# Mamba-2 decay matrices built as an offset minus an absolute difference, with Abs and Exp in place in PSUM

## What is computed

```python
def _ssd(xh, dt, A, Bm, Cm):
    cum = jnp.cumsum(dt * A, axis=1)
    diff = cum[:, :, None, :] - cum[:, None, :, :]
    decay = jnp.where(mask[None, :, :, None], jnp.exp(diff), 0.0)
    scores = jnp.einsum('bln,bsn->bls', Cm, Bm)[..., None] * decay * dt[:, None, :, :]
    return jnp.einsum('blsh,bshp->blhp', scores, xh)

def _mamba2(x, Win, Wconv, bconv, dt_bias, A_log, D, gn_w, Wout):
    zxbcdt = x @ Win                       # z, x, B, C, dt
    xBC = silu(causal_conv(...))           # x 128 wide, B and C 16 wide
    dt = softplus(zxbcdt[..., -NHEADS:] + dt_bias)
    y = _ssd(xh, dt, A, Bm, Cm) + rev(_ssd(rev(xh), rev(dt), A, rev(Bm), rev(Cm)))
    y = y + D * xh
    y = _rmsnorm(y.reshape(b, l, DIN) * silu(z), gn_w)
    return y @ Wout
```

## Time and profile before

| | |
|---|---|
| time, median of 3 runs | 2949.18 us (2942.47 to 2951.99) |
| profiled execution | 2953.49 us, of it 2951.5 us span from first to last instruction |
| granted TensorE clock, mean | 0.857 of full speed |
| busy: TensorE, VectorE, ScalarE, GpSimd | 2153.9, 1981.8, 1744.2, 1079.7 us |
| the first block begins | 904.9 us into the span |
| the eighth block | 2680.4 to 2929.1 us |

### The profile page before, as it was taken

One profiled execution on the slowest core, in us unless ns is written; L12 is line 12 of the kernel. 1 busy time (PEld: TensorE's weight loads), 2 busy tenths in 40 slices (PEclk: granted clock), 3 DMA queues, 4 the chain that ended last, 5 costly groups with the idle time before them and its releaser, 6 DMA issues. The chain is left out here.

```text
span 2951.5 us, 64266 instructions
## 1 busy us (share of the span) xinstructions
PE 2153.9 (73%) x26182; PEld 1100.1 (37%) x26182; DVE 1981.8 (67%) x2779; ACT 1744.2 (59%) x2811; POOL 1079.7 (37%) x827
## 2 busy tenths in 40 slices
PE   4277777776774887698688588658857886885886
PEld 3022222222221553354255245325524542552553
DVE  2587888888877566565666656565765666666564
ACT  1266766766653575477367457536754773674574
POOL 0044444444451343244045235304522531451342
PEclk6588888888896998799799799869978988997998
DMA  4000000000001111110111111011111101111111
GB/s 133 0 0 1 0 1 0 1 0 0 1 0 29 32 34 28 35 33 15 44 38 26 38 27 40 15 31 32 34 36 26 42 15 39 33 25 30 32 34 31
DMA packets 96695, 74.59 MB, mean 25 GB/s; under 512 B 69392, under 2 KB 77584, under 8 KB 95120
## 3 DMA queue, kind: packets, MB, share of 16 engines
q1 hardware_dynamic: 96400, 70.48, 10.0%
HBM read 20.62 MB, written 8.39 MB: 10 GB/s over the span
## 5 line engine op out<-in xcount | busy, mean ns | idle before, releaser
L892 POOL TENSOR_TENSOR SQ<-SQ 128x512 f32<-128x512 f32 x344 | 467.2, 1360 | 708.4 <-ACT SQ L811 425.1
L859 POOL TENSOR_TENSOR Y<-Z 128x512 f32<-128x512 f32 x256 | 330.8, 1292 | 531.6 <-DVE Z L1096 297.7
L807 ACT ACTIVATE O<-bank 128x512 f32<-128x512 f32 x512 | 304.3, 594 | 210.2 <-PE bank L571 207.5
L1293 DVE TENSOR_TENSOR SQ<-bank,O 128x512 f32<-128x512 f32 x344 | 236.2, 689 | 163.8 <-issue 118.8
L571 PE MATMUL bank<-SS,work 32*128 32x512 bf16 x512 | 203.7, 398 | 169.3 <-ACT O L807 168.2
L892 POOL TENSOR_TENSOR SQ<-O,SQ 128x512 f32<-128x512 f32 x168 | 226.9, 1350 | 254.8 <-PE bank L592 185.7
L1096 DVE TENSOR_TENSOR_SCAN Z<-bank,SS 128x512 f32<-128x512 f32 x256 | 311.0, 1215 | 0.5
L536 PE MATMUL bank<-folded_weights,work 128*64 128x128 f32 x4096 | 300.1, 292 | 0.0
L463 PE MATMUL bank<-Y,constants 128*128 128x512 f32 x512 | 295.5, 662 | 6.2 <-DVE bank L1104 4.6
L592 PE MATMUL bank<-folded_weights,work 128*32 128x64 f32 x8192 | 287.3, 230 | 11.3 <-POOL SQ L892 10.8
L512 PE MATMUL bank<-XP,block_weights 128*128 128x512 f32 x256 | 156.9, 725 | 174.3 <-DVE Z L1227 174.3
(11 more groups left out here) (271 smaller groups left out, 3990.2 us busy)
## 6 DMA issues: line engine op xcount, KB each, us to landing
work<-XP SPq DMA_DIRECT2D x256, 134.0 KB
work<-extra SPq DMA_DIRECT2D x768, 8.0 KB
decay_cols_kept<-extra SPq DMA_DIRECT2D x48, 128.0 KB, 1.8
SS<-decay_cols_kept SPq DMA_DIRECT2D x384, 16.0 KB
block_weights<-callw SPq DMA_DIRECT2D x8, 735.0 KB, 4.4
Z<-state_sel SPq DMA_DIRECT2D x1, 2048.0 KB, 13.2
out<-O SPq DMA_DIRECT2D x2, 1024.0 KB, 8.5
constants<-consts SPq DMA_DIRECT2D x1, 1347.5 KB, 6.1
```

The costliest lines, as they stand in the source:

```text
L807: A(D2C[u % 2], bank[2], ACT.Copy).then_inc(sg("d2_copied"), 1)
L859: g.tensor_tensor(hc[t_ % 4], hs[t_ % 4], c_copy[t_ % 4], ALU.mult).then_inc(sg("s1_hc"), 1)
L892: g.tensor_tensor(MM[u % 2].rearrange("p (h l) -> p h l", l=L), DK[u % 3].rearrange("p (h l) -> p h l", l=L), GM[(u // 8) % 2][:, 64 * (u ...
L1293: v.tensor_tensor(DK[u % 3], bank[u % 2], D2C[u % 2], ALU.min).then_inc(sg("decay_least"), 1)
```

## The change

A decay exponent, the smaller of two sums, is written as an offset minus an absolute difference. The first matmul puts the difference in a bank; ScalarE takes Abs in place there; a second matmul accumulates the offset onto it; ScalarE takes Exp of the negative in place; VectorE multiplies the bank with the scores into SBUF. So the copy (L807), the minimum (L1293) and all of GpSimd's part of the blocks go. Three banks and three product tiles rotate. Only three arrays (M, G, C) are split, with all roundings on ScalarE (`round_high`, `round_mid`) and all differences on VectorE (`take_high`, `take_mid`).

The weights of block c + 1 are folded during block c, into a second buffer. z is projected whole ahead of the loop through five banks and copied to SBUF by ScalarE (`copy_z`); its tanh and product are taken in the loop, for each group in slots 0 and 1, through bank 7. The scores are 16 matmuls of 32 rows x 64 columns in place of 8 of 64 x 128. The first group's x, B and C are projected and gated ahead of the loop. ScalarE issues six of the first group's DMAs.

```diff
+                def decay_matmul(u, k):
+                    h = slice(32 * k, 32 * k + 32)
...
+                    return mm(bank[u % 3], LHS[r][h, 2 * a:2 * a + 128], cols[h, :, :], start=(k == 0), stop=(k == 1),
+                              tile_position=(32 * k, 0), skip_group_check=True)
+                def distance(u):
...
+                    if u >= 3:
+                        pe.wait_ge(sg("multiplied"), c * L + u - 2)
+                    decay_matmul(u, 0).then_inc(sg("distances"), 1)
+                def decay_logs(u):
+                    pe.wait_ge(sg("distance_abs"), c * L + u + 1)
+                    decay_matmul(u, 1).then_inc(sg("decay_logs"), 1)
...
+                project_bc(0)
+                project_x(0, 0)
+                project_x(0, 1)
+                for i in range(5, 16):
+                    z(i)
+                pe.wait_ge(sg("z_copied"), c * 16 + 16)
                 for tau in range(FIRST, LAST):
                     if 0 <= tau - 1 < L:
                         y(tau - 1)
+                    if 0 <= tau + 2 < L:
+                        decay_logs(tau + 2)
                     if 0 <= tau + 3 < L:
-                        decay_logs(tau + 3)
-                    for i in Z_SLOTS.get(tau, ()):
-                        z(i)
+                        distance(tau + 3)
```

The scores on TensorE, and the first lines of ScalarE's loop:

```diff
                     for u in range(8):
-                        last = mm(bank[6][:, 64 * u:64 * u + 64], BB[0:64, 128 * u:128 * u + 128],
-                                  C2[0:64, 64 * u:64 * u + 64], start=True, stop=True, skip_group_check=True)
+                        for b in range(NB):
+                            h, a = slice(32 * b, 32 * b + 32), slice(64 * u, 64 * u + 64)
+                            last = mm(bank[6][64 * b:64 * b + 64, a], BB[h, a], C2[h, a], start=True, stop=True,
+                                      tile_position=(32 * b, 64 * b), skip_group_check=True)
```

```diff
                     u = tau + 2
                     if 0 <= u < L:
-                        act.wait_ge(sg("decay_logs2"), c * L + u + 1)
...
-                        A(D2C[u % 2], bank[2], ACT.Copy).then_inc(sg("d2_copied"), 1)
...
-                        A(DK[u % 3], DK[u % 3], ACT.Exp).then_inc(sg("decay_ready"), 1)
+                        act.wait_ge(sg("decay_logs"), c * L + u + 1)
+                        A(bank[u % 3], bank[u % 3], ACT.Exp, scale=-1.0).then_inc(sg("decay_ready"), 1)
+                    u = tau + 3
                     if 0 <= u < L:
+                        act.wait_ge(sg("distances"), c * L + u + 1)
+                        A(bank[u % 3], bank[u % 3], ACT.Abs).then_inc(sg("distance_abs"), 1)
```

VectorE, where `gate_z` now stands ahead of `gate_x`:

```diff
-                        dve.wait_ge(sg("decay_logs1"), c * L + u + 1)
-                        dve.wait_ge(sg("d2_copied"), c * L + u + 1)
...
-                        v.tensor_tensor(DK[u % 3], bank[u % 2], D2C[u % 2], ALU.min).then_inc(sg("decay_least"), 1)
-                    for i in Z_SLOTS.get(tau, ()):
+                        dve.wait_ge(sg("decay_ready"), c * L + u + 1)
...
+                        v.tensor_tensor(MM[u % 3].rearrange("p (h l) -> p h l", l=L),
+                                        bank[u % 3].rearrange("p (h l) -> p h l", l=L),
+                                        GM[(u // 8) % 2][:, 64 * (u % 8):64 * (u % 8) + 64].unsqueeze(1).broadcast_to(
+                                            [128, 8, L]), ALU.mult).then_inc(sg("multiplied"), 1)
+                    i = z_due(tau)
+                    if i is not None:
                         gate_z(i)
                     for offset, work_ in ((-3, gate_x), (5, gate_y)):
```

More of the change, by code:

```diff
@@ L276, in rows_of_decay @@
[L276 to L282, removed]
+                        sp.wait_ge(sg("decay_logs"), c * L + 8 * (g - 1))
@@ L286, in call @@
                 sp.wait_ge(sg("zeroed"), 1)
[L287 to L291, removed]
+                keep(0, "M")
+                decay_rows(sp, 0, 0, "M")
+                keep(1, "G")
+                sp.wait_ge(sg("decay_stored_M"), (c + 1) * 48)
+                cols_of_decay(0, 0, "M")
+                sp.wait_ge(sg("decay_stored_G"), (c + 1) * 48)
+                cols_of_decay(0, 1, "G")
+                sp.wait_ge(sg("split_C"), c + 1)
                 rows_of_decay(1)
@@ L625, in call @@
                         g = every(tau, 8, offset, NGROUP)
-                        if g is not None:
+                        if g is not None and (g > 0 or offset != -8):
                             work_(g)
@@ L801, in call @@
+                hbbc = folded(c)[7]
+                tanh_bc(0)
+                tanh_x(0)
+                act.wait_ge(sg("split_C"), c + 1)
+                decay_rows(act, 0, 1, "C")
+                for i in range(5, 16):
+                    copy_z(i)
                 for tau in range(FIRST, LAST):
@@ new lines, in call @@
+                    g = every(tau, 8, -7, NGROUP)
+                    if g is not None and g > 0:
+                        tanh_bc(g)
+                    i = z_due(tau)
+                    if i is not None:
+                        act.wait_ge(sg("z_copied"), c * 16 + 16)
+                        if i >= 1:
+                            act.wait_ge(sg("z_ready"), c * 16 + i)
+                        if i >= 4:
+                            act.wait_ge(sg("scaled"), c * 8 + i // 2 - 1)
+                        A(bank[7], Z2[:, z_at(i)], ACT.Tanh, scale=0.5).then_inc(sg("z_tanh"), 1)
@@ L1141, in call @@
+            for piece in range(8):
+                fold(0, piece)
             def call(m, n, d, c):
@@ L1297, in call @@
                         k = every(tau, 4, offset, 16)
-                        if k is not None:
+                        if k is not None and (k > 0 or offset != -3):
                             work_(k)
@@ L1301, in call @@
                         g = every(tau, 8, offset, NGROUP)
-                        if g is not None:
+                        if g is not None and (g > 0 or offset > -5):
                             work_(g)
```

363 lines of the change are left out of this document (177 added, 186 removed).

## The result

The changed kernel takes **3032.05 us** (3029.24 to 3037.4, 4 runs), the kernel before 2950.59 (2942.47 to 2953.03, 4 runs) beside it: ratio **1.0285**, 95% interval 1.0271 to 1.0299. It is slower by about 81 us. The forecast was 2998, in a range of 2895 to 3050: right in sign, 34 us too low, and 2 us above the range of 2960 to 3030 that it gave even odds.

A forecast was written before the change was run, and what follows sets the result against it. A group was taken as TensorE's work plus waits for ScalarE, 18.5 + 2.4 = 20.9 us. Per block -9.9 + 16.9 - 1.4 = +5.6, eight +44.8, plus 4.5 once: 2949 + 49 = 2998 us, range 2895 to 3050.

The forecast's parts named there:

- The chain: Loop, slots 1 to 2: TensorE's projection of x waits for gate_x behind gate_z, 4.2 us a group, 3.6 in one piece.
- the table loads: Loop, slots 5 to 7: TensorE waits 0.6, 0.4 and 0.4, together 1.4 us where 1.72 + 0.66 stood.
- The clock: Loop: low level of 1.2 GHz after the new wait in every group, costing 1.6 us, 7 times a block.
- rival (3): Worse: Abs and Exp at 0.66 and scores without gain, or a low clock that stays longer: 3049 us, chance 0.12.
- Rival (1): The clock holds and the low level doesn't follow the new wait: 2909 us, 2877 with best scores; chance 0.28.
- The scores: Loop, TensorE: 16 half-width matmuls take 1.6 us a group where 8 took 2.0; at best 1.1.
- In-place Abs and Exp: Loop, ScalarE, PSUM to PSUM: 0.46 us per instruction, from a 552 ns row; upper bound 0.66 us.
- The preamble: Block start to first product: 49.1 us where it was 59.0, -9.9 us a block, bounds -6 to -12.
- The start of block 0: Block 0's weights are folded ahead of everything, costing 4.5 us once.
- Last group and drain: End of a block: faster product on VectorE and shorter last additions, 31.3 us for 32.7, -1.4.
- the loop's +16.9: Seven groups from first to 57th product: 173.8 us with the low clock against 156.9, +16.9 a block.
- The sum: Whole kernel: +5.6 a block, eight +44.8, and 4.5 once, +49; against the median 2998 us.

The follow-up runs named there:

- gate_x_first: Changed kernel with VectorE doing gate_x and gate_y ahead of gate_z in each step: 2762.17 us, ratio 0.9367 to the kernel before.
- filled_wait: Changed kernel with 80 small zero-weight matmuls added in TensorE's wait of slot 2, ahead of the projection of x: 2936.47 us, ratio 0.9961.
- sums_later: gate_x_first with only the sums of squares one slot later: 2718.3 us, ratio 0.9218 to the kernel before.
- loop_moved: gate_x_first with sums of squares one slot later, taps of B and C split over slots 0 and 1, gate_z one step later: 2647.58 us, ratio 0.8979.
- tanh_z_first: Changed kernel with ScalarE's tanh of z ahead of tanh and bias of B and C: 2923.16 us, ratio 0.9911.
- copies_early: gate_x_first with five of ScalarE's eleven late copies of z moved up among the splits of C: 2751.62 us, ratio 0.933.

## Why the prediction came out as it did

**The chain** was right in place, cause and size. The forecast had a wait of 3.6 us in one piece, 56 times, released by `gate_x`, with `gate_z` of slot 1 waiting for a tanh of z; measured 3.52, 56 times. gate_x_first took it away and the slowdown with it. The 0.58 of slot 1, and 0.58 + 0.37 + 0.34 at the table loads, stand where 0.6 and 0.6 + 0.4 + 0.4 were forecast.

**The clock** was right in kind, a little low in size: 1.6 us a group forecast, 1.9 measured in two ways in the eighth block, up to 2.3 in others. It is not once per group: behind the first, the groups of the block last 24.7 to 24.9 us with one low stretch of 3.4 us, and 26.0 to 26.2 with two, which the prediction had only under rival (3). Without the clock the seven groups come to 173.6 - 13.3 = 160.3 (forecast 162.6), with it to 173.6 (forecast 173.8). That the two last agree to 0.2 us is luck: the waits and the work were 2.3 too long and the clock's part 2.1 too short, and the mean over the blocks is 175.0. The Trainium skill, "TensorE: Matmul & The Clock Gate", section "What's actually happening", says that activity releases the throttle; filled_wait agrees, at 13.4 us less for more work. Rival (1), that the clock holds, is excluded by the windows of the changed kernel itself.

**The scores** were mis-sized: 1.6 us taken, 1.15 in the row, the best bound of 1.1 nearly met. Over the seven groups of eight blocks this is some 25 us in the kernel's favour, and more than the 2.3 a block that the loop without the clock was too long.

**In-place Abs and Exp** took 574 and 579 ns where 552 was taken, and a start every 0.48 to 0.50 us for 0.46. The Trainium skill, "ScalarE: Activation LUTs", section "What ACT_TABLE_LOAD costs", gave an estimated 613 ns, above both; the measured durations decide.

**The preamble** was right: -9.9 forecast, -9.0 in the eighth block (-10.3 in the mean over the others). The start of block 0 was delayed by 6.1 us (911.0 for 904.9) for 4.5 forecast.

**What failed is the step "Last group and drain", 31.3 for 32.7, -1.4.** It had two faults. The first is in the reading: I took the 156.9 us of the earlier trace rows for the stretch from first product to the 57th. Measured between those products it is 161.4, and the last part 28.2, not 32.7. So the loop's +16.9 was really +12.2, by a base 4.5 too low. This moved 4.5 us from one part to the other and left their sum as it was: on the right base the forecast is +12.4 for the loop and +3.1 for the last part.

The second fault is that the last part grew by 5.3, to 33.5 where 31.3 was forecast. By the rows above, in the eighth block: from the 57th product to the sums of squares 11.8 us for 9.6 (11.6 still in gate_x_first); from there to the output projection 6.0 for 3.5, because the block's last Exp now stands ahead of the table load and waits 2.17 us for its matmul; the output projection 3.63 for 1.98, at the low clock; and from its end to `y_ready` 1.0 less, 12.1 for 13.1. That is 2.2 + 2.5 + 1.65 - 1.0. The forecast had only the last of these. Most of the growth stays with gate_x_first (33.1 in the mean over the blocks, where the changed kernel has 33.5 and the kernel before 28.5), so the chain isn't its main cause. sums_later, where the last Exp's matmul no longer stands behind the sums of squares, has 31.1: 2.0 us a block hang on that order. No run moved the Exp itself, and the other 2.6 are read from the rows, not shown by an experiment.

**The sum.** In the mean over the blocks the change costs 9.1 us each ((78.6 - 6.1) / 8), forecast 5.6: 28 us of the error. Of the 3.5 us a block, 2.2 are the last part (33.5 for 31.3) and 1.2 the loop (175.0 for 173.8). Block 0 adds 1.6. The rest is that I took 4.3 us off, the distance of the profiled execution from the median, which the changed kernel's runs did not have.

## What to carry to other kernels

In an engine's in-order program, look at every instruction that was put in front of an older one and ask when its input comes: a `gate_z` of 0.69 us cost 3.5 us a group because it waited for a tanh that the instruction behind it didn't need. Price such a stall with its clock: here 2.84 us of wait brought 1.9 us of slow matmuls with it. And judge a new form of the computation only after its order is tuned: as delivered it was 2.9% slower, with four changes of order (loop_moved) 10% faster, while one of them made the old form 2.8% slower, and two 4.5%.

## What the hardware showed that I had not expected

Adding 80 matmuls to each group made the kernel 96 us faster, by the clock alone. A stall of 2.2 us in dense work (tanh_z_first) was enough for the low level in many groups, where the 0.68 us wait of gate_x_first left the clock at 1.00 over seven groups of the eighth block. Sixteen score matmuls of 32 rows and 64 columns took 1.15 us where eight of 64 x 128 took 2.00: the two of a pair, on different rows and columns of the array, start 6 to 7 ns apart in the trace, and a pair takes 0.14 us where one wide matmul takes 0.25. And making TensorE's work start earlier can put it into a low stretch: in copies_early the scores came earlier and took 1.97 us.
